# Causal-mask matmuls in attention, GpSimd products in halves and one state's weighing moved to VectorE

## What is computed

```python
# layer 0, attention: 16 heads of 16, causal, ALiBi bias
attn = einsum('bhqd,bhkd->bhqk', q, k) * scale + alibi_bias   # -inf above the diagonal
out  = einsum('bhqk,bhkd->bhqd', softmax(attn), v)
# layer 1, state space: 512 channels, 16 states, per time step
h = exp(dt * A) * h + (dt * u) * B_t        # h, A: [512, 16]
y = sum over the 16 states of h * C_t
```

## Time and profile before

| | |
|---|---|
| time, median of 3 runs | 4169.15 us (4162.0 to 4174.61) |
| the profiled execution | 4161.75 us, span 4160.0 us |
| busy over the span | PE 79%, PEld 36%, DVE 87%, ACT 56%, POOL 64% |
| attention | 260.8 to 1266 us |
| scans of the state space | 2123 to 3945 us |
| granted PE clock, mean of the span | 0.896 |

### The profile page before, as it was taken

How to read it: one execution, slowest core, us unless ns; L and a number is a source line. 1 busy time by engine, 2 the same in 40 slices (tenths; PEclk the granted TensorE clock), 3 DMA queues, 4 the chain that set the end, 5 groups by cost and what they waited for, 6 DMA issues and landing times. The chain is left out here.

```text
span 4160.0 us, 60548 instructions
## 1 busy us (share of the span) xinstructions
PE 3305.8 (79%) x21452; PEld 1518.2 (36%) x21452; DVE 3599.1 (87%) x6205; ACT 2324.5 (56%) x4310; POOL 2658.1 (64%) x2217
## 2 busy tenths in 40 slices
PE   5979999999994999999667776777777777776477
PEld 3623333333332555555322222222232322222166
DVE  5768888888864999999369999999999999999967
ACT  5626666666673344444366666666666666666422
POOL 1102222222231888888369999999999999999723
PEclk8969999999996999999878888888888888888689
DMA  4894555565622111110112222211222222221132
GB/s 146 279 182 68 73 80 80 80 86 69 88 35 83 36 44 45 44 48 30 35 45 62 62 65 63 64 47 59 68 64 63 64 66 62 63 57 57 41 94 84
DMA packets 274955, 299.55 MB, mean 72 GB/s; under 512 B 35583, under 2 KB 205686, under 8 KB 274646
## 3 DMA queue, kind: packets, MB, share of 16 engines
q1 hardware_dynamic: 274654, 295.68, 30.9%
HBM read 210.22 MB, written 84.51 MB: 71 GB/s over the span
## 5 line engine op out<-in xcount | busy, mean ns | idle before, releaser
L1708 POOL TENSOR_TENSOR d_dBu<-d_dtu,d_Bn 128x2048 f32<-128x2048 f32 x256 | 1182.0, 4640 | 0.1
L1550 ACT ACTIVATE d_dA<-d_dt,d_decay 128x512 f32<-128x512 f32 x1024 | 690.8, 687 | 391.1 <-DVE d_h L1789 388.3
L746 ACT ACTIVATE b_P<-b_pT 128x512 f32<-128x512 f32 (+1 forms) x1120 | 571.4, 576 | 328.8 <-PE b_pT L654 328.5
L1789 DVE TENSOR_TENSOR_SCAN d_h<-d_dA,d_last_h,d_dBu 128x512 f32<-128x512 f32 x512 | 615.7, 1263 | 18.3 <-PE d_y L1451 7.9
L776 DVE CUSTOM_DVE_ANT_0 b_pS<-b_pS,mask_qk 128x512 f32<-128x512 f32 (+3 forms) x1024 | 581.1, 617 | 50.1 <-PE b_pS L664 45.1
L1789 DVE TENSOR_TENSOR_SCAN d_h<-d_dA,d_dBu 128x512 f32<-128x512 f32 x512 | 586.0, 1203 | 38.7 <-ACT d_dA L1550 33.0
L664 PE MATMUL b_pS<-KS,QS 99*128 99x512 bf16 (+3 forms) x1536 | 471.5, 339 | 71.6 <-DVE b_Gc L776 47.2
L626 POOL TENSOR_SCALAR_AFFINE_SELECT b_P<-b_P 128x128 f32<-128x128 f32 (+2 forms) x608 | 191.4, 321 | 506.1 <-ACT b_P L746 493.2
L654 PE MATMUL b_pT<-QS,KS 118*128 118x512 bf16 (+3 forms) x1536 | 450.2, 330 | 19.5 <-ACT b_gT L730 16.3
L1697 POOL TENSOR_TENSOR d_h<-d_h,d_Cn 128x2048 f32<-128x2048 f32 x80 | 361.7, 4521 | 132.3 <-ACT d_Cn L1560 114.2
L1434 PE MATMUL d_C<-d_bc,d_pick 96*128 96x512 bf16 x256 | 115.6, 452 | 378.8 <-DVE d_h L1796 378.3
(11 more groups left out here) (309 smaller groups left out, 6023.5 us busy)
## 6 DMA issues: line engine op xcount, KB each, us to landing
d_Bn<-scratch_bs SPq DMA_DIRECT2D x128, 512.0 KB, 4.9
scratch_parts<-a_part SPq DMA_DIRECT2D x48, 512.0 KB, 4.1
QS<-scratch_parts SPq DMA_DIRECT2D x192, 128.0 KB, 7.3
KS<-scratch_parts SPq DMA_DIRECT2D x192, 128.0 KB, 7.8
scratch_v<-a_v SPq DMA_DIRECT2D x16, 1024.0 KB, 7.6
V<-scratch_v SPq DMA_DIRECT2D x32, 512.0 KB, 11.7
a_x<-in_L_attn_x_dram SPq DMA_DIRECT2D x16, 512.0 KB, 7.7
scratch_o<-b_O SPq DMA_DIRECT2D x16, 512.0 KB, 10.1
```

Of the source, the lines that this page charges most:

```text
L746: act.activation(t[:, heads[0]:heads[-1] + 1, c * CH:c * CH + w], pT[:, place % RING, 0:len(heads) * w].rearrange("p (h w) -> p h w", w=w) ...
L1550: act.activation(dA[:, m % 2, :], dt[:, c.k % 2, m, :], ACT.Exp, scale=decay[:, m, n:n + 1]).then_inc(dA_d, 1)
L1708: pool.tensor_tensor(product(c, n), dtu[:, c.k % 2, :, :], Bn[:, n // BG % 2, n % BG, :].unsqueeze(1).to_broadcast([P, MD, CH]), ALU.mult) ...
L1789: dve.tensor_tensor_scan(h[:, n % HS, m, :], dA[:, m % 2, :], product(c, n)[:, m, :], start, ALU.mult, ALU.add).then_inc(scanned, 1)
```

## The change

- In `attend`, a piece with the diagonal that holds more than one head is masked on PE: behind each head's score matmul a second matmul (identity, bf16, times a new 128x128 bf16 tile `mask_bf` that holds the mask) adds the mask into the same PSUM columns. DVE then reduces the whole piece with one `tensor_reduce`. Pieces with one head keep the fused instruction.
- ACT runs `lift_maxima` ahead of `lift` at slot 4.
- DVE's `normalise` is split: `invert` (the reciprocal) behind slot 8, the product behind slot 10.
- In `state_space`, state 8 leaves `POOL_C`: DVE weighs it in slot 9, ACT no longer copies C_8, and its sum on PE goes from slot 11 to slot 10.
- POOL's product is issued in two halves of two tiles (128x1024). Each half waits only for the scans of the tiles that it overwrites, three states back, and DVE's scans of tiles 0 and 1 wait for the first half only. The counts of `dBu_d` double for all that wait for it.

```diff
@@ setup
+            pool.memset(K["mask_bf"][:, :], 0.0).then_inc(id_set, 1)
...
+            for t in ("mask_qk", "mask_bf"):
+                pool.affine_select(out=K[t][:, 0:P], in_=K[t][:, 0:P], compare_op=ALU.is_ge, fill=MASKED,
+                                   base=0, pattern=[[1, P]], channel_multiplier=-1).then_inc(id_done, 1)
@@ attend, scores_for_max
-                    last = pe.matmul(p, QS[0:R0 + NPART, g, h, qt * P:(qt + 1) * P], KS[0:R0 + NPART, g, h, first:first + w], start=True, stop=True)
+                    last = pe.matmul(p, QS[0:R0 + NPART, g, h, qt * P:(qt + 1) * P], KS[0:R0 + NPART, g, h, first:first + w], start=True, stop=(c > 0 or len(heads) == 1))
+                    if c == 0 and len(heads) > 1:
+                        last = pe.matmul(p[:, 0:P], K["ident_bf"][:, :], K["mask_bf"][:, :], start=False, stop=True)
@@ attend, scalar engine
                     if j == G_AT:
+                        if joined is not None:
+                            lift_maxima(joined)
                         if turned is not None:
                             lift(turned)
-                        if joined is not None:
-                            lift_maxima(joined)
@@ attend, vector engine
+            def invert(u):
+                wait(dve, o_tr, u.times(1, 1))
+                dve.reciprocal(rden[:, :, :], turned_rows()[:, :, :, HD]).then_inc(r_done, 1)
...
-                        if c == 0:
-                            for n, h in enumerate(heads):
-                                last = dve.tensor_tensor_reduce(...)
+                        if c == 0 and len(heads) == 1:
+                            last = dve.tensor_tensor_reduce(...)
...
                     if j == 8 and turned is not None:
+                        invert(turned)
+                    if j == 10 and turned is not None:
                         normalise(turned)
@@ state_space
-POOL_C = (0, 3, 6, 8, 11)
+POOL_C = (0, 3, 6, 11)
...
-                wait(pool, scanned, c.times(NS * MD, MD * (n + 1 - BS)))
-                pool.tensor_tensor(product(c, n), dtu[:, c.k % 2, :, :], Bn[:, n // BG % 2, n % BG, :].unsqueeze(1).to_broadcast([P, MD, CH]), ALU.mult).then_inc(dBu_d, 1)
+                for j in range(2):
+                    wait(pool, scanned, c.times(NS * MD, MD * (n - BS) + 2 * j + 2))
+                    pool.tensor_tensor(product(c, n)[:, 2 * j:2 * j + 2, :], dtu[:, c.k % 2, 2 * j:2 * j + 2, :],
+                                       Bn[:, n // BG % 2, n % BG, :].unsqueeze(1).to_broadcast([P, 2, CH]), ALU.mult).then_inc(dBu_d, 1)
...
-                wait(dve, dBu_d, c.times(NS, n + 1))
                 for m in range(MD):
+                    if m % 2 == 0:
+                        wait(dve, dBu_d, c.times(2 * NS, 2 * n + m // 2 + 1))
```

More of the change, by code:

```diff
@@ L141, in _ @@
             pool.memset(K["mask_qk"][:, :], 0.0).then_inc(id_set, 1)
-            pool.wait_ge(id_set, 3)
+            pool.memset(K["mask_bf"][:, :], 0.0).then_inc(id_set, 1)
+            pool.wait_ge(id_set, 4)
             for t in ("ident", "ident_bf"):
@@ L145, in _ @@
                                    base=0, pattern=[[-1, P]], channel_multiplier=1).then_inc(id_done, 1)
-            pool.affine_select(out=K["mask_qk"][:, 0:P], in_=K["mask_qk"][:, 0:P], compare_op=ALU.is_ge, fill=MASKED,
-                               base=0, pattern=[[1, P]], channel_multiplier=-1).then_inc(id_done, 1)
+            for t in ("mask_qk", "mask_bf"):
+                pool.affine_select(out=K[t][:, 0:P], in_=K[t][:, 0:P], compare_op=ALU.is_ge, fill=MASKED,
+                                   base=0, pattern=[[1, P]], channel_multiplier=-1).then_inc(id_done, 1)
             q_edge, k_edge, own = edge[:, 0, :], edge[:, 1, :], (NROW + 2 * NPART) * EDGE
@@ L159, in _ @@
                                base=EDGE - 1 - own, pattern=[[-1, T]], channel_multiplier=EDGE).then_inc(edge_set, 1)
-            pool.wait_ge(id_done, 3)
+            pool.wait_ge(id_done, 4)
         @block.scalar
@@ L754, in _, with turned_rows @@
             dve.wait_ge(gc_set, 1)
+            def turned_rows():
+                return pO[:, :].rearrange("p (t h c) -> p t h c", h=HG, c=VW)
+            def invert(u):
+                wait(dve, o_tr, u.times(1, 1))
+                dve.reciprocal(rden[:, :, :], turned_rows()[:, :, :, HD]).then_inc(r_done, 1)
             def normalise(u):
[L758 to L761, removed]
+                g, o = u.k % NG, turned_rows()
                 wait(dve, r_done, u.times(1, 1))
@@ L773, in step @@
                         maxima = Gc[:, m.k % 2, c, :].rearrange("p (h t) -> p h t", t=QT)
-                        if c == 0:
-                            for n, h in enumerate(heads):
-                                last = dve.tensor_tensor_reduce(out=pS[:, j % RING, n * w:(n + 1) * w], in0=pS[:, j % RING, n * w:(n + 1) * w], in1=K["mask_qk"][:, 0:w],
-                                                                scale=-1.0, scalar=-MASKED, op0=ALU.add, op1=ALU.min, accum_out=maxima[:, h, qt:qt + 1])
+                        if c == 0 and len(heads) == 1:
+                            last = dve.tensor_tensor_reduce(out=pS[:, j % RING, 0:w], in0=pS[:, j % RING, 0:w], in1=K["mask_qk"][:, 0:w],
+                                                            scale=-1.0, scalar=-MASKED, op0=ALU.add, op1=ALU.min, accum_out=maxima[:, heads[0], qt:qt + 1])
                         else:
@@ L788, in _ @@
             units(dve, step)
+            invert(LAST)
             normalise(LAST)
@@ L1381, in spread_next @@
                 if c is not None:
-                    wait(sp, dBu_d, c.times(NS, BG * (g - 1)))
+                    wait(sp, dBu_d, c.times(2 * NS, 2 * BG * (g - 1)))
                     spread_b(c, g)
@@ L1404, in step @@
                         if c is not None:
-                            wait(sp, dBu_d, c.times(NS, NS - BG + BG * g))
+                            wait(sp, dBu_d, c.times(2 * NS, 2 * (NS - BG + BG * g)))
                         spread_b(q, g)
@@ L1845, in gate_y @@
                 wait(dve, silu_z, e.times(1, 1))
-                wait(dve, dBu_d, e.times(NS, NS))
+                wait(dve, dBu_d, e.times(2 * NS, 2 * NS))
                 dve.tensor_tensor(dtu[:, e.k % 2, :, :], y[:, :, :], z[:, e.k % 2, :, :], ALU.mult).then_inc(yz_d, 1)
@@ L2119, in kept @@
             return {n: stack.enter_context(nc.sbuf_tensor(n, shape, dt)) for n, (shape, dt) in shapes.items()}
-        K = kept(ctx, {"ident": ([P, P], F32), "ident_bf": ([P, P], BF16), "mask_qk": ([P, CH], F32),
+        K = kept(ctx, {"ident": ([P, P], F32), "ident_bf": ([P, P], BF16), "mask_qk": ([P, CH], F32), "mask_bf": ([P, P], BF16),
                        "sa0": ([P, KD, B], F32), "ca0": ([P, KD, B], F32), "sb1": ([P, KD, B], F32), "cb1": ([P, KD, B], F32)})
```

## The result

The changed kernel takes **4126.8 us** (median of 4 runs, 4124.9 to 4131.1) beside 4166.9 for the kernel before: ratio 0.9908, 95% interval 0.9896 to 0.9920, so 0.9% faster. That lies in the range of the prediction (4088 to 4150); the forecast, 4116 from 4169 or -53 us, was 13 us too good. Its two stages were wrong in opposite ways and by more than that, so that the sum came out in the range is in part luck. The profiled executions span 4160.0 and 4123.2 us, -36.8.

A forecast was written before the change was run, and what follows sets the result against it. PE was taken as nearly the bound in attention, DVE as the bound in the state space. Attention -40 and state space -11 (35 - 7 - 39) gave -51 us, 4111 to 4118, stated as 4116 us; range 4088 to 4150.

The forecast's parts named there:

- Masking on PE: Attention: shorter DVE reductions start PE's next unit earlier, the eight new matmuls included; 0.4 us a unit gained.
- Order on ACT: Attention, place 7: copying the maxima before `lift` frees the place about when PE wants it; 0.4 us a unit gained.
- Split of `normalise`: Attention, slots 8 to 12: slot 9's bank is released earlier, so PE waits less at slot 12; 0.45 us a unit gained.
- Rival A: Attention: PE gets ahead of DVE's banks again, only the unit's end gains, 10 us; time 4148 us, chance 0.17.
- sign of being wrong: Attention: the prediction called itself wrong if PE's idle stayed above 1.5 us a unit.
- Weighing: State space: DVE weighs state 8 in each of 16 chunks, paid in full because DVE is the bound; +35 us.
- Products no longer waited for: State space, slot 9: with halves the first scans start on half a product; -7 us.
- `split_rest`: State space, slot 9: it waits for at most one half product, 1.9 us instead of 4.5, in 15 chunks; -39 us.
- The waits for ACT: State space: DVE's 28 us of waits for ACT were left unchanged.
- the cover: State space, slot 9: the new weighing covers ACT's exponentials for the next chunk as `split_rest` did; no change in waits.
- Rival B: State space: the relief of `split_rest` is eaten, returning at most 20 us; time 4137 to 4147 us, chance 0.14.
- Rival C: State space: POOL's next half goes ahead of waiting `split_rest`, about 8 us each; 4210 us, chance 0.07 including another rival.

The follow-up runs named there:

- k4: Changed kernel with all diagonal masks back on DVE, no mask matmuls, and state 6 also weighed by DVE: attention 996.8 us, scans 1825.8 us.
- c4: Changed kernel with the product behind slot 9, all diagonal masks on DVE, and a useless ACT copy in slot 9: attention 977.9 us, scans 1813.3 us.
- k3: Changed kernel with `lift` ahead of `lift_maxima` again, and POOL's weighings and `step_input` product also in halves: attention 1000.4 us, scans 1803.3 us.
- c3: Changed kernel with product behind slot 9, `lift` ahead of `lift_maxima`, state 8 on POOL and whole products (state-space control): attention 981.7 us, scans 1822.6 us.
- k2: Changed kernel with the `normalise` product behind slot 8, and POOL's products whole again: attention 978.5 us, scans 1823.0 us.
- k1: Changed kernel with the `normalise` product behind slot 9, and state 8 back on POOL: attention 967.5 us, scans 1811.8 us.
- d2: Changed kernel with reciprocal behind slot 7, product behind slot 8, state 8 back on POOL, `split_rest` in slot 10: attention 974.4 us, scans 1829.1 us.
- d4: Changed kernel with product behind slot 9, and the state space of the kernel before with `split_rest` in slot 10: attention 967.6 us, scans 1842.4 us.
- c2: Changed kernel with PE's first values matmuls moved from slot 12 to 13, and `split_rest` in slot 10: attention 977.9 us, scans 1802.5 us.

## Why the prediction came out as it did

**Attention: -40 forecast, -16.2 measured.** Three terms were summed, and the experiments price each by itself:

- Masking on PE: forecast -12.8 (0.4 us x 32). Measured 10.3 twice (k4, c4). The eight mask matmuls cost what the rows said: in the trace after, eight alternating short matmuls run from 602.78 to 603.25, 0.059 us each.
- Order on ACT: forecast -12.8. Measured 13.9 and 14.1 (k3, c3).
- Split of `normalise`: forecast -14.4 (0.45 x 32). Measured **+8.0** (the changed kernel against k2). This is the step that failed: the forecast charged the product behind slot 10 with 0.2 us a unit on slot 11's bank, and with nothing for what waits for the product itself. It counted PE's wait for the banks on either side of slot 12, and that part was right: 1.05 us fell to 0.31. It left out that the product releases the output tile, so that moving it two slots later makes PE's values late. The wait is not new in the code, `values` has always waited for `o_done`; in the trace before it never showed, because the product ended in time. Splitting was not the mistake, the place was: with the product behind slot 9, attention is 967.6 against 978.5 for both behind slot 8, so -10.9 of the -14.4; slot 10 in place of 9 costs 19. The prediction asked of each added wait who stands behind it, but not of each *moved* instruction who waits for its end.

The sum is consistent: -10.3 - 13.9 + 8.0 = -16.2. Rival A (the waits move on, 10 us left) named the right kind of event in the wrong place: it was not PE getting ahead of the banks. The prediction's sign of being wrong, PE's idle still above 1.5 us a unit, did not show this failure: it is 1.25, the two waits above.

**State space: -11 forecast, -21.8 measured.** Weighing +35, as forecast (+35.5 by the page's groups, 433.4 against 397.9). Products no longer waited for, -7.5, as forecast. `split_rest` was the mis-sized term: forecast 1.9 us each, -39; measured 18.7 us for 15 instead of 68.5, so 1.25 us on average and -50. It does not meet a half at random, but arrives at one of two distances ahead of a boundary, chunk by chunk in turn, as the two lines above show. The prediction placed one chunk (wait 0.9, found 0.9) and then took the mean of a uniform wait all the same; in the other kind of chunk the wait is 0.1. The waits for ACT grew by 6, which the prediction had left at nothing; as they are 36 in the control c3 too, which has neither edit, they can't be put down to what the change does. Counted from start to start of DVE's instructions, first to last scan: weighings +34.4, products -7.8, `split_rest` -49.8, ACT +6.3, waits for PE's sums -3.3, `modulate` -0.9, together -21.1 of the -21.8.

One statement behind the forecast proved more important than it was given: that the new weighing gives ACT's and PE's work the cover that `split_rest` had given. k1, d2 and d4 show what happens without it. Of the 3.8 us by which `split_rest` was longer than its 0.68, up to 2.8 were covering PE's sums (waits of 2.16 us in k1, 2.81 in d4); the change gains because it puts 2.2 us of useful work in that place *and* makes what is left short. Neither edit does it alone.

Rival B (ACT takes the relief back) happened in a small measure at most, the 6 us above. Rival C, that the second half gets the port ahead of a waiting `split_rest`, fell in the changed kernel: its longest case there is 2.2 us. It was seen in other arrangements (d2, c2, k1); why DVE was passed over there and got in at the first boundary elsewhere is open. The Trainium skill ("SBUF — State Buffer", Who interferes with whom) says that a VectorE instruction with two SBUF inputs is held off for the whole of a GpSimd instruction that reads SBUF; all the rows here agree, `split_rest` (both inputs in SBUF, long beside POOL) against the weighing L1809 (one of them in PSUM, the same 2.26 us throughout) above all. The same section of the Trainium skill says that issue order decides who blocks. By the starts in the profile that would put a waiting `split_rest` ahead of the next half; the row of 9.21 us in d2, started at 3092.97 and passed over by halves from 3094.67 on, does not bear this out, and when POOL's halves were issued no view shows.

Two small sums of the prediction are off: the chances for "faster" add up to 0.88, not 0.87, and the 2 us between 4118 and 4116 have no term. Neither matters to the result.

## What to carry to other kernels

Before an instruction is moved later, list every wait for its semaphore, also those that cost nothing in the trace: slack that is used up does not show. A stall on the bounding engine may be the cover of another engine's work; removing it pays only if useful work takes its place, which is why the two edits here are worth 22 to 27 us together, and apart 6 to 11 (the halves) and nothing (state 8). Where two engines meet at a fixed phase, place the meeting in each kind of iteration instead of taking a mean.

## What was not expected of the hardware

- A copy of 128x12 elements in SBUF (`carry`, L1828 before) takes 1.98 us in the median, since it too ends only when POOL's instruction does; the memset of the same tile, which takes its place in every other chunk, takes 0.07 us beside POOL's product, and `bn_stats` on 128x256 takes 0.41 us, as elsewhere.
- Cutting POOL's work finer is not better by itself: a pair of halves takes 0.14 us longer than the whole (k3), and there is no gain where DVE arrives in the last part of the instruction.
- A waiting DVE instruction does not always get in at POOL's next boundary: 9.21 and 6.61 us beside halves of 2.33 (d2), 4.20 (c2), 6.92 (k1).
- A bank wait of 0.3 us a unit in c2 stands in no PE row's bracket, since the end of the matmul before covers it; the starts and the weight load show it.
